# One kernel of a whole small network: in the local transformer layers, the LayerNorm scale and a product on GpSimd and TensorE, a softmax exponential on ScalarE and two pieces on VectorE stand in another order

## The reference, cut to what matters

```python
def attn_layer(x, Wqkv, qs, ksc, Wo):            # 16 heads of 64, windows of 32 tokens
    qkv = x @ Wqkv
    q, k, v = ...
    q = l2norm(q) * qs;  k = l2norm(k) * ksc      # per head
    q = q * cos * scale + rotate_half(q) * sin * scale
    k = k * cos * inv + rotate_half(k) * sin * inv
    out = local_attention(q, k, v)                # softmax over own and previous window
    return out @ Wo
def ffn_layer(x, g, bln, W1, b1, W2, b2):
    mu = x.mean(-1, keepdims=True)
    var = ((x - mu) ** 2).mean(-1, keepdims=True)
    xn = (x - mu) / jnp.sqrt(var + 1e-05) * g + bln
    hg = xn @ W1 + b1
    a, gate = jnp.split(hg, 2, -1)
    return a * jax.nn.gelu(gate, approximate=False) @ W2 + b2
for i in range(DEPTH):
    x = attn_layer(shift_tokens(x), Wqkv[i], q_scale[i], k_scale[i], Wo[i]) + x
    x = ffn_layer(shift_tokens(x), ln_g[i], ln_b[i], W1[i], b1[i], W2[i], b2[i]) + x
```

## Time and profile before

| | |
|---|---|
| median of 3 runs | 7309.48 us (7299.09 to 7326.49) |
| the profiled execution | 7311.83 us, of which the span of its instructions 7309.8 us |
| PE busy | 5516.9 us (75%) |
| DVE busy | 4515.6 us (62%) |
| ACT busy | 2992.9 us (41%) |
| POOL busy | 3221.5 us (44%) |
| mean granted TensorE clock | 0.868 of full |

### The profile page before, as it was taken

One profiled execution on the slowest core, in us unless ns is written; L12 is line 12 of the kernel. 1 busy time (PEld: TensorE's weight loads), 2 busy tenths in 40 slices (PEclk: granted clock), 3 DMA queues, 4 the chain that ended last, 5 costly groups with the idle time before them and its releaser, 6 DMA issues. The chain is left out here.

```text
span 7309.8 us, 148489 instructions
## 1 busy us (share of the span) xinstructions
PE 5516.9 (75%) x55030; PEld 3401.9 (47%) x55030; DVE 4515.6 (62%) x5698; ACT 2992.9 (41%) x4895; POOL 3221.5 (44%) x1391
## 2 busy tenths in 40 slices
PE   4737776185876858588888888888888888888886
PEld 3524444021222212255655565555555555555654
DVE  4352113241423233688888888888888888888885
ACT  0002222032221313355555555555555555555553
POOL 0000000000000000577777777777777777777773
PEclk8658888587887968799999999999999999999997
DMA  0000100301001010111111112111111111111111
GB/s 17 0 7 20 32 26 20 50 1 25 2 13 14 0 26 1 58 31 31 31 50 32 29 29 53 30 29 33 50 29 29 32 50 32 29 30 38 31 30 41
DMA packets 153433, 202.64 MB, mean 28 GB/s; under 512 B 40904, under 2 KB 79698, under 8 KB 151614
## 3 DMA queue, kind: packets, MB, share of 16 engines
q1 hardware_dynamic: 153312, 201.04, 12.0%
HBM read 63.67 MB, written 11.53 MB: 10 GB/s over the span
## 5 line engine op out<-in xcount | busy, mean ns | idle before, releaser
L99 POOL TENSOR_TENSOR ln_post_rstd<-ln_post_var,neg_half 128x8 f32<-128x8 f32 x16 | 26.5, 1655 | 2919.3 <-DVE ln_post_var L80 2919.3
L1597 POOL TENSOR_TENSOR d_rnorm<-d_sq_clip,neg_half 128x32 f32<-128x32 f32 x192 | 1234.3, 6429 | 82.1 <-DVE d_sq_clip L1460 81.9
L1590 POOL TENSOR_TENSOR d_qk_swap<-d_qk_raw,d_rot 128x512 f32<-128x512 f32 x768 | 1150.1, 1528 | 14.4 <-ACT d_qk_raw L1312 14.4
L1150 PE MATMUL d_ring<-d_wqkv,d_xin 128*128 (+1 forms) x1536 | 765.7, 632 | 265.0 <-ACT d_qk_raw L1312 195.2
L1574 POOL TENSOR_TENSOR d_probs_n<-d_probs,d_prec 128x1024 f32<-128x1024 f32 x192 | 544.1, 2834 | 934.9 <-DVE d_prec L1485 934.9
L866 DVE TENSOR_REDUCE c_mx<-c_ps 128x1 f32<-128x512 f32 (+3 forms) x768 | 417.0, 556 | 772.7 <-PE c_ps L737 768.8
L834 ACT ACTIVATE c_pt<-c_ps 128x512 f32<-128x512 f32 (+1 forms) x640 | 354.3, 554 | 1119.8 <-PE c_ps L752 1117.8
L1443 DVE TENSOR_TENSOR d_qk_part<-d_qk_raw,d_rot 128x1024 f32<-128x1024 f32 x384 | 782.3, 2056 | 46.8 <-issue 27.6
L766 PE MATMUL c_ps<-c_pt,c_vg 128*32 128x512 f32 (+3 forms) x1536 | 630.7, 508 | 4.7 <-DVE c_ots L871 4.7
L1150 PEld LDWEIGHTS d_ring<-d_wqkv,d_xin 128*128 128x128 f32 x1536 | 274.1, 193 | 615.5 <-issue 463.2
L1203 PE MATMUL d_op<-d_band,d_v 128*64 128x128 f32 x6144 | 458.0, 312 | 0.0
(11 more groups left out here) (258 smaller groups left out, 9684.6 us busy)
## 6 DMA issues: line engine op xcount, KB each, us to landing
d_band<-d_own_t SPq DMA_DIRECT2D x768, 64.0 KB
d_band<-d_prev_t SPq DMA_DIRECT2D x576, 64.0 KB
d_v_prev<-d_v SPq DMA_DIRECT2D x191, 128.0 KB, 2.3
b_w<-in_L_ffn_w SPq DMA_DIRECT2D x64, 256.0 KB, 3.4
d_band_prev<-d_prev_t SPq DMA_DIRECT2D x192, 64.0 KB
d_wqkv<-in_L_ffn_Wqkv SPq DMA_DIRECT2D x6, 1536.0 KB
c_kp<-c_k_scratch SPq DMA_DIRECT2D x30, 256.0 KB
c_qp<-c_q_scratch SPq DMA_DIRECT2D x24, 256.0 KB
```

What stands on the lines that cost most here:

```text
L1150: eng.matmul(ring[c % 3][:, :], xin[p][:, :], wqkv[:, bass.ds(par, 1), c * 512:(c + 1) * 512].rearrange("p l n -> p (l n)"), start=True, s ...
L1590: mm = eng.tensor_tensor(qk_swap[:, which, :, out:out + hd], qk_raw[:, which, :, src:src + hd], rot[:, bass.ds(par, 1), which, 1, bass.ds( ...
L1597: eng.tensor_tensor(rnorm[:, :], sq_clip[:, :], neg_half[:, 0:2 * HEADS], ALU.pow).then_inc(rn_ready, 1)
```

## The change

Four pieces change their place; no instruction is added or removed. (1) GpSimd makes `rstd` and `rstd_diag` at the head of the even slot, ahead of `probs_n`, not behind it. (2) TensorE's product that spreads them stands behind `attended`, and VectorE's `xn`, which reads it, behind `squares`. (3) The exponential of the even slot goes into the next odd slot of ScalarE, between the copies `raw(1)` and `square(0)`. (4) On VectorE the multiplication by `rnorm` (the norms) stands ahead of `hid`, not behind it.

```diff
@@ TensorE
                         turn(3)
-                    if even:
-                        eng.wait_ge(diag_ready, k - 2)
-                        eng.matmul(ff[:, 0, :], ones[:, :], rstd_diag[:].rearrange("p u t -> p (u t)"), start=True, stop=True).then_inc(bc_ready, 1)
...
                     if u == 0 and g:
                         attended()
+                    if even:
+                        eng.wait_ge(diag_ready, k - 2)
+                        eng.matmul(ff[:, 0, :], ones[:, :], rstd_diag[:].rearrange("p u t -> p (u t)"), start=True, stop=True).then_inc(bc_ready, 1)
                     if s:
                         scores()
@@ ScalarE
-                    def exponent():
-                        eng.wait_ge(sub_ready, n)
+                    def exponent(m):
+
+                        eng.wait_ge(sub_ready, m + 1)
                         eng.activation(probs[:], probs[:], ACT.Exp, scale=8.0).then_inc(exp_ready, 1)
...
                         raw(1)
+                    if f and u == 1:
+                        exponent(n - 2)
+                    if a:
                         square(0)
...
-                        exponent()
+                        exponent(n - 1)
...
-                    if s and u == 0:
-                        exponent()
@@ VectorE
                     if f and u == 0:
                         total()
+                    if s:
+                        eng.wait_ge(rn_ready, n)
+                        heads = qk_part[1 - p][:].rearrange("p a h d -> p (a h) d")
+                        eng.tensor_tensor(heads, heads, rnorm[:, :].unsqueeze(2).broadcast_to((P, 2 * HEADS, DH)),
+                                          ALU.mult).then_inc(rope_ready, 1)
                     if late:
...
-                    if s:
-                        eng.wait_ge(rn_ready, n)
...
                     if f:
                         blocks()
+                    if a:
+                        squares()
                     if even:
...
-                    if a:
-                        squares()
@@ GpSimd
+                    if even:
+                        eng.wait_ge(ve_ready, k - 2)
+                        eng.tensor_tensor(rstd[:, :], var_eps[:, :], neg_half[:, 0:2], ALU.pow)
...
                     if f:
                         eng.wait_ge(rec_ready, n - 1)
...
-                    if even:
-                        eng.wait_ge(ve_ready, k - 2)
-                        eng.tensor_tensor(rstd[:, :], var_eps[:, :], neg_half[:, 0:2], ALU.pow)
```

More of the change, by code:

```diff
@@ L1497, in slot @@
                                                      op0=ALU.add, op1=ALU.mult).then_inc(hid_ready, 1)
-                    if s:
-                        eng.wait_ge(rn_ready, n)
-                        heads = qk_part[1 - p][:].rearrange("p a h d -> p (a h) d")
-                        eng.tensor_tensor(heads, heads, rnorm[:, :].unsqueeze(2).broadcast_to((P, 2 * HEADS, DH)),
-                                          ALU.mult).then_inc(rope_ready, 1)
                     if f and u == 1:
@@ L1569, in slot @@
                     even = u == 0 and live(6)
+                    if even:
+                        eng.wait_ge(ve_ready, k - 2)
+                        eng.tensor_tensor(rstd[:, :], var_eps[:, :], neg_half[:, 0:2], ALU.pow)
+                        eng.drain()
+                        eng.tensor_tensor(rstd_diag[:], ident[:, :].unsqueeze(1).broadcast_to((P, 2, P)), rstd[:, :].unsqueeze(2).broadcast_to((P, 2, P)),
+                                          ALU.mult).then_inc(diag_ready, 1)
                     if f:
@@ L1575, in slot @@
                                           ALU.mult).then_inc(pn_ready, 1)
-                    if even:
-                        eng.wait_ge(ve_ready, k - 2)
-                        eng.tensor_tensor(rstd[:, :], var_eps[:, :], neg_half[:, 0:2], ALU.pow)
-                        eng.drain()
-                        eng.tensor_tensor(rstd_diag[:], ident[:, :].unsqueeze(1).broadcast_to((P, 2, P)), rstd[:, :].unsqueeze(2).broadcast_to((P, 2, P)),
-                                          ALU.mult).then_inc(diag_ready, 1)
                     if a:
```

## The result

| | before | changed kernel |
|---|---|---|
| median | 7317.98 us (4 runs, 7299.09 to 7330.76) | 7398.64 us (4 runs, 7397.96 to 7418.66) |
| the profiled execution | 7311.83 us, span 7309.8 | 7398.24 us, span 7396.4 |
| ratio of the times | | 1.0119, 95% interval 1.0089 to 1.0149 |

The account below looks back on a forecast made before the run. The prediction took a chain from engine to engine, not a full engine, to bound the kernel. The profiled 7311.8 us plus 20 for the chain and 57 for TensorE's clock gave 7389, said as 7390; range 7285 to 7470.

Parts of the forecast that it names:

- What bounds it: Whole pair of slots: no engine is full; a chain going from engine to engine sets the 43.34 us per pair.
- Part 1: Even slot, `rstd` first on GpSimd: the first `qk_swap` gets ahead of the second cosine, which ends 1.10 us later.
- Part 2: Even slot: PE loses its 2.37 us wait, but the values' copy waits for the `v_prev` DMA; the chain keeps 0.47 us.
- Part 3: ScalarE: exponential behind two copies ends 1.0 us later after the value copy; total at t 25.25 against 25.04, +0.2 us.
- Part 4: VectorE, norms ahead of `hid`: gain up to 2.2 us ends in a wait for the exponential; nothing on the path.
- The rest of the pair unchanged: From total to residual 11.09 us, to `center` 1.16, to the end of `var_eps` 6.09 more, all as before.
- TensorE's clock, +57 us: Output projection: clock falls behind PE's moved pause, 0.75 us in most pairs, 0.6 in the mean, over 95 pairs.
- The +20 us of the chain: Pair grows from 43.38 to 43.59 us without the clock; by 95 pairs, +20 us.
- no clock fall: Rival, 25%: the clock does not fall on the output projection; 7332 us.
- The swap does not get ahead: Rival, 13%: swap stays behind the second cosine and the clock holds; total 0.9 us earlier, 7226 us.
- The clock falls for longer: Rival, 10%: the fallen clock costs 2 us per pair, 7520 us; at one us in the mean 7425.
- The power holds `rotated` up: Rival, 2%: GpSimd's power delays VectorE's `rotated`, starting at 18.8 rather than 15; total 1.9 us later, 7490 us.

Follow-up runs that it names:

- gap_kept: Changed kernel with a spare, unread GpSimd power added between `probs_n` and the first swap in the even slot; 7269.54 us, 0.9947 of the kernel before.
- vprev_first: Changed kernel with the DMA into `v_prev` issued ahead of the eight band DMAs in even slots; 7099.39 us, 0.9713 of the kernel before.
- before_vprev_first: Kernel before with only the DMA into `v_prev` issued ahead of the band DMAs in even slots; 7302.55 us, ratio 0.9994.
- exp_back: Changed kernel with the even slot's exponential back at the end of that slot; 7339.34 us, 1.0036 of the kernel before.
- norms_back: Changed kernel with the norms back behind `hid` on VectorE; 7400.98 us, 1.0117 of the kernel before.
- filler: Changed kernel with two unread 128x512 products in TensorE's pause ahead of the output projection; 7324.88 us, 1.0020 of the kernel before.
- only_bc_moved: Kernel before with only the product of `rstd_diag` moved behind `attended` and `xn` behind `squares`; 7285.85 us, ratio 0.9956.
- rstd_back: Changed kernel with `rstd` and its diagonal back behind `probs_n` on GpSimd; 7273.48 us, 0.9939 of the kernel before.

## Why the prediction was right

- **What bounds it:** a chain, not an engine. Confirmed: between the first and the last `var_eps` VectorE and PE are each busy for 82% of the time (83% and 85% before), and the time moves with single waits.
- **Part 1, the second cosine loses its turn, +1.10 us:** right in mechanism and size (t 9.26 against 9.27, the swap 2.26 us long), and shown by gap_kept, which restores only the gap.
- **Part 2, of PE's 2.37 us the chain keeps 0.47:** right for the changed kernel, where the copy ran at 18.10 with the DMA last. The 0.47 is the gain over pairs with a slow `attended`; the median moved by 0.43, the mean by 0.04. vprev_first and before_vprev_first show that the DMA is the limit in the one kernel and not in the other.
- **Part 3, the exponential 1.0 us later relative to the copy:** right in size; exp_back moved the total by 0.97. The total came at 25.15 against 25.25. But against the mean of the kernel before it is 0.56 later, not 0.2.
- **Part 4, norms worth nothing:** right, by norms_back, 7400.98 against 7398.64.
- **The rest of the pair unchanged:** right in the median: with the clock restored by filler, from the total to the residual it took 11.10 us (11.11 before). Not right in the mean. The kernel before had 13 pairs in which the second cosine of the odd slot lost its turn; the changed kernel has one, because W2 is done before the total. So this part became shorter, by 0.19 us to the residual and 0.21 behind it (filler against before). The step failed the other way in exp_back and only_bc_moved, where the median grew by 1.2 us.
- **TensorE's clock, +57 us:** right in place and mechanism, the term that was mis-sized. I took 0.6 us a pair: 0.75 in four pairs of five. It came in 82 of 95, and where it falls it costs 1.69 less the 0.86 of slack, 0.83: 68 us, and filler measured 69.2.
- **The +20 us of the chain:** 13.3 by filler, and that it came so near is partly luck. It is the balance of a total that came 0.56 us later and of 0.40 us won back behind it, and the prediction had 0.2 of the one and nothing of the other. Together with the clock 82.5 us over the 95 pairs, where the two terms were 77.
- **The rivals:** "no clock fall" is excluded by 491 ns and a clock of 0.68, and filler shows what it would have been, 7325 where the rival said 7332. "The swap does not get ahead" is gap_kept's case; it gave 7270 rather than the 7226 of the rival, since the clock did not hold (457 ns a projection product there). "The clock falls for longer" is excluded: each fall cost 0.83 us, not 2. "The power holds `rotated` up" is excluded: `rotated` took 2283 ns in the mean of 192, with `rnorm` beside it.

The Trainium skill (SBUF — State Buffer, section "Who interferes with whom") lets the order of issue decide who blocks. The runs agree in two cases: a cosine loses its turn once a swap is issued first, and `rnorm` takes 7.43 us when `rotated` is issued 0.14 us ahead of it, 5.43 when it is not. They differ in the other direction: in the pair above GpSimd's power ran from 5021.09 to 5026.52, and `rotated`, issued in the middle of it at 5022.25, took 2.28 us all the same.

What stays open: why the clock stays up in 13 of the 95 pairs (in 40 with rstd_back) and falls in the others at a like pause; that was not tried. That turns go by how long each has waited is argued from rows, and gap_kept shows only the consequence.

## What to carry to other kernels

A wait that you take away hands the chain to the next one behind it, so look for that one in the same slot before moving anything: here a DMA queued ninth stood right behind a 2.37 us wait, each edit alone gave 0.4% or nothing, and both together 3.2%. Before you let one pair stand for the mean, see whether the pairs are of one kind. Where two engines take turns at memory, a short instruction that keeps one of them away may be worth more than the time that it takes. Shortening a chain lengthens pauses of TensorE elsewhere; price them at the lower clock where they fall, and see whether there is slack behind them.

## What the runs showed of the hardware that I had not expected

- A product of 16 matmuls took 3.69 us at the full clock and 5.38 us behind a pause of 2.57 us, in 82 of 95 pairs. The same pause in rstd_back was followed by the full clock in 40 of 95.
- Two spare matmuls of 128x512 (1.88 us for both) in that pause brought 74 us, 1.0%.
- GpSimd's power over 128x2 took 0.70 us where no cosine ran and 1.67 us beside one, and the cosines beside it were not longer (4.05 us for two).
- Where the addition ahead of a cosine started 0.22 us later after the total, the cosine took 2.29 us in place of 1.27: turn-taking made a delay cost nearly five times its size.
